# Softmax reciprocals turned once and spread by two transfers, in a cross-attention kernel with a planned order

## The reference

```python
q, k, v = layernorm(x) @ Wq + bq, ctx @ Wk + bk, ctx @ Wv + bv   # 16 heads of 32
sim  = q k^T * 32**-0.5, masked
attn = softmax(sim, axis=-1)
x1   = x + (attn @ v) @ Wo + bo
hn   = layernorm(x1)
p    = softmax(hn @ Ws + bs)                # 4096 tokens x 8 experts
for each expert e: rows = top 512 of p[:, e]
    y = gelu(hn[rows] @ W1[e] + b1[e]) @ W2[e] + b2[e]
    x1[rows] += y * p[rows, e]
```

## Time and profile before

| | us |
|---|---|
| Median of 3 timed runs | 1693.4 |
| The runs | 1683.93, 1697.06, 1693.4 |
| The profiled execution | 1688.73 |
| Its span | 1686.9 |
| Its mean granted TensorE clock | 0.982 |

### The profile page before, as it was taken

How to read it: one execution, slowest core, us unless ns; L and a number is a source line. 1 busy time by engine, 2 the same in 40 slices (tenths; PEclk the granted TensorE clock), 3 DMA queues, 4 the chain that set the end, 5 groups by cost and what they waited for, 6 DMA issues and landing times.

```text
span 1686.9 us, 22363 instructions
## 1 busy us (share of the span) xinstructions
PE 1601.5 (95%) x7847; PEld 1164.9 (69%) x7847; DVE 1113.7 (66%) x1950; ACT 978.3 (58%) x2115; POOL 301.6 (18%) x396
## 2 busy tenths in 40 slices
PE   7999999999999999999976899999999999999997
PEld 5556566666666666666543687888888888888885
DVE  7676968868778697786845667775455545454543
ACT  5898898988989889798863123222232323232321
POOL 6220311312213122130300100102020202020100
PEclk9999999999999999999987999999999999999999
DMA  5543654635446364463611231525253425333430
GB/s 176 172 136 112 188 142 139 189 100 183 145 137 191 95 188 145 133 188 94 189 54 63 83 118 56 164 88 156 100 156 99 134 99 154 103 112 123 109 114 25
DMA packets 131271, 217.27 MB, mean 129 GB/s; under 512 B 17116, under 2 KB 51056, under 8 KB 131160
## 3 DMA queue, kind: packets, MB, share of 16 engines
q1 hardware_dynamic: 114520, 173.23, 32.6%
q0 software_dynamic: 16640, 42.61, 9.3%
HBM read 157.45 MB, written 57.82 MB: 128 GB/s over the span
## 4 chain that ended last, share of the span: by engine, by line
PE 82%; DVE 7%; DMA 4%; ACT 4%; issue 2%; POOL 0%; SPq 0%; DVEq 0%; POOLq 0%; ACTq 0%
PE ps_gen L886 9%; PE ps_gen L887 8%; PE ps_gen L888 8%; PE ps_gen L2067 7%; PE ps_gen L2069 7%; PE ps_gen L2068 7%; PE ps_gen L1903 7%; PE ps_gen L1871 6%; PE ps_att L1914 6%; PE ps_gen L1853 3%; PE ps_gen L1854 3%; PE ps_gen L1855 3%; ACT ps_gen L1278 2%; PE ps_gen L1930 2%; PE ps_gen L1931 2%
## 5 line engine op out<-in xcount | busy, mean ns | idle before, releaser
L1474 DVE TENSOR_REDUCE nmax<-ps_gen 128x1 f32<-128x512 f32 x512 | 330.0, 683 | 78.6 <-PE ps_gen L1871 76.7
L1290 ACT ACTIVATE p_ring<-ps_gen,keep_scale 128x512 f32<-128x512 f32 x512 | 337.7, 701 | 57.8 <-PE ps_gen L1903 47.7
L1278 ACT ACTIVATE ps_gen<-ps_gen,nmax 128x512 f32<-128x512 f32 x512 | 343.3, 680 | 28.6 <-DVE nmax L1474 28.1
L1347 ACT ACTIVATE gel<-ps_gen,b_cols 128x512 f32<-128x512 f32 x128 | 88.3, 690 | 448.8 <-PE ps_gen L888 448.7
L1735 DVE TENSOR_TENSOR gel_lo<-gel,gel_hi 128x512 fp32r<-128x512 f32 x126 | 87.3, 692 | 281.6 <-ACT gel_hi L1348 281.6
L1903 PE MATMUL ps_gen<-qst,kst 99*128 99x512 f32 x512 | 196.8, 425 | 10.7 <-DMA qst<-by_row 9.5
L1871 PE MATMUL ps_gen<-kst,qst 97*128 97x512 f32 x512 | 186.6, 423 | 17.9 <-DMA qst<-qk_rows 7.8
L886 PE MATMUL ps_gen<-hT_hi,w_hi 128*128 128x512 f32 x512 | 202.2, 395 | 0.1
L888 PE MATMUL ps_gen<-hT_hi,w_lo 128*128 128x512 f32 x512 | 199.5, 390 | 0.0
L887 PE MATMUL ps_gen<-hT_lo,w_hi 128*128 128x512 f32 x512 | 199.4, 389 | 0.0
L2067 PE MATMUL ps_gen<-w_hi,gel_hi 128*128 128x512 f32 x504 | 198.1, 393 | 0.0
(11 more groups left out here) (218 smaller groups left out, 2671.2 us busy)
## 6 DMA issues: line engine op xcount, KB each, us to landing
w_raw<-in_L_ffn_W SPq DMA_DIRECT2D x128, 512.0 KB, 5.0
kst<-qk_rows SPq DMA_DIRECT2D x93, 256.0 KB, 4.0
qst<-qk_rows SPq DMA_DIRECT2D x93, 256.0 KB, 3.8
x_in<-in_x POOLq DMA_DIRECT2D x60, 256.0 KB, 3.9
out_x<-x_in SPq DMA_DIRECT2D x32, 256.0 KB, 3.2
qk_rows<-kT_hi SPq DMA_DIRECT2D x31, 256.0 KB, 2.0
qk_rows<-kT_lo SPq DMA_DIRECT2D x31, 256.0 KB, 3.5
qk_rows<-qT_hi SPq DMA_DIRECT2D x31, 256.0 KB, 2.0
```

What stands on the lines that cost most here:

```text
L1278: e.activation(psum[:, :], psum[:, :], ACT.Exp, bias=nmax[g % 2][:, c], scale=-1.0, accum_out=den[g % 2][:, c]).then_inc(drained_sem("max" ...
L1290: e.activation(p_ring[n % NP_][:, :], ps("score", g, kt, h)[:, :], ACT.Exp, scale=keep_scale[:, b:b + 1]).then_inc(drained_sem("score", g, ...
L1474: e.tensor_reduce(nmax[g % 2][:, h * TB + t:h * TB + t + 1], ps("max", g, h, t)[:, :], AX.X, ALU.min).then_inc(s_min, 1)
```

## The change

- `recip` ends with VectorE's reciprocals of 128 x 16. `rden_wide` and GpSimd's spread are gone.
- `rden` is one transpose of 128 x 16 to 16 x 128. ScalarE, not VectorE, copies it, as 16 rows, to `rden_rows` (partitions 64 to 79 of `by_row`).
- SP gets two new steps: `den_out` stores the 16 rows in HBM (`den_rows`, 8 KB), `den_in` loads them into `rden_b` (128 x 512), where each of 4 heads' rows of 512 goes to 32 partitions. `den_in` waits for `den_out` to land and for the division of the group before.
- `divide` multiplies `ps_att` by `rden_b` and waits for `den_in`. It also takes over the wait for the split of the group before.
- `piece_in` is due at `NG - 1` and needs the last stacks and the last maximum rows in the plan. In SP's program its own semaphore waits are the same.
- Planner: some costs are 1% higher, maximum rows are reckoned at 3.2 instead of 2.6 us, `LOOK` is 0, and nearly all due times and lags are new.

```diff
-           "att": (1.105, 1.15), "v": (2.74, 2.94), ...
+           "att": (1.120, 1.17), "v": (2.78, 2.98), ...
-    "pe": {"proj": (0.693, 0.89), "max": (0.231, 0.43), "rows": (0.109, 0.31), "rden": (0.436, 0.63), ...
+    "pe": {"proj": (0.700, 0.90), "max": (0.235, 0.43), "rows": (0.109, 0.31), "rden": (0.109, 0.31), ...
-    "pool": {"rows_lo": (1.050, 2.60), "recip": (0.560, 0.66), ...
+    "pool": {"rows_lo": (1.050, 3.20), ...
+             "den_out": (0.360, 2.40), "den_in": (0.360, 3.60), ...
-LOOK = 0.023
+LOOK = 0
...
-K_AT = ((0.24, 0.248), (-0.055, 0.281), (0.094, 0.256), (-0.698, -0.096))
-Q_AT = ((0.472, 0.472), (0.34, 0.351), (0.109, 0.318), (0.248, 0.412))
-MAX_AT = ((0.124, 0.67), (0.036, 0.694), (-0.083, 0.753), (0.309, 0.742))
-ROWS_AT, RECIP_AT, RDEN_AT, OSPLIT_AT, ATT_AT = 0.132, 0.197, 0.833, -0.55, 0.042
+K_AT = ((0.261, 0.362), (-0.04, 0.247), (0.044, 0.207), (-0.373, -0.096))
+Q_AT = ((0.442, 0.468), (0.192, 0.352), (0.222, 0.42), (0.384, 0.511))
+MAX_AT = ((0.015, 0.674), (-0.097, 0.585), (-0.024, 0.954), (0.091, 0.741))
+ROWS_AT, RECIP_AT, RDEN_AT, OSPLIT_AT, ATT_AT = -0.78, 0.558, 0.153, -0.175, 0.093
...
-            p.add("pool", ("recip", g), g + RECIP_AT, [("dve", "recip", g), ("pe", "rden", g - 1)])
-        p.add("dve", ("rden", g), g + RDEN_AT, [("pe", "rden", g), ("dve", "osplit_lo", g - 1)], frees=("rden", g))
+        p.add("act", ("rden", g), g + RDEN_AT, [("pe", "rden", g), ("sync", "den_out", g - 1)], frees=("rden", g))
+        p.add("sync", ("den_out", g), g + RDEN_AT, [("act", "rden", g), ("sync", "den_in", g - 1)])
+        p.add("sync", ("den_in", g), g + RDEN_AT, [("sync", "den_out", g), ("dve", "divide", g - 1)])
...
-        p.add("dve", ("divide", g), g + 1, [("pe", "att", g, KT - 1), ("dve", "rden", g)])
+        p.add("dve", ("divide", g), g + 1, [("pe", "att", g, KT - 1), ("sync", "den_in", g), ("dve", "osplit_lo", g - 1)])
...
+    stacked = [("sync", "stack_" + k, w, NG - 1) for k in ("hi", "lo") for w in "kq"] + [("pool", "rows_lo", NG - 1)]
     for n in range(3):
-        p.add("sync", ("piece_in", n), NG - 2, done)
+        p.add("sync", ("piece_in", n), NG - 1, done + stacked)
...
+                elif kind == "den_out":
+                    g, = at
+                    on.wait_ge(*drained("rden", g))
+                    if g > 0:
+                        on.wait_ge(s_den_in, 16 * g)
+                    e.dma_start(den_rows, rden_rows).then_inc(s_den_out, 16)
+
+                elif kind == "den_in":
+                    g, = at
+                    on.wait_ge(s_den_out, 16 * (g + 1))
+                    on.wait_ge(s_nrm, g)
+                    src = den_rows.rearrange("(h d t) n -> h d (t n)", d=1, t=TB).to_broadcast([HG, DH, S])
+                    e.dma_start(rden_b[:, :], src).then_inc(s_den_in, 16)
...
+                elif kind == "rden":
+                    g, = at
+                    on.wait_ge(*full("rden", g))
+                    if g > 0:
+                        on.wait_ge(s_den_out, 16 * g)
+                    e.activation(rden_rows, ps("rden", g)[0:HG * TB, 0:P], ACT.Copy).then_inc(drained_sem("rden", g), 1)
...
-                    e.tensor_copy(att_n[:, :], ps("rden", g)[:, :]).then_inc(drained_sem("rden", g), 1)
...
-                    e.tensor_tensor(att_n[:, :], ps_att[:, :], att_n[:, :], ALU.mult).then_inc(s_nrm, 1)
+                    e.tensor_tensor(att_n[:, :], ps_att[:, :], rden_b[:, :], ALU.mult).then_inc(s_nrm, 1)
...
-                    on.wait_ge(s_rden_wide, g + 1)
-                    for t in range(TB):
-                        last = e.transpose(ps("rden", g)[:, t * P:(t + 1) * P], rden_wide[:, t, :], ident[:, :])
-                    last.then_inc(full_sem("rden", g), 1)
+                    on.wait_ge(s_rden, g + 1)
+                    e.transpose(ps("rden", g)[0:HG * TB, 0:P], rden[:, :], ident[:, :]).then_inc(full_sem("rden", g), 1)
```

More of the change, by code:

```diff
@@ L351 @@
 COST = {
[L352 to L355, removed]
+    "pe": {"proj": (0.700, 0.90), "max": (0.235, 0.43), "rows": (0.109, 0.31), "rden": (0.109, 0.31), "score": (0.235, 0.43),
+           "att": (1.120, 1.17), "v": (2.78, 2.98), "turn": (0.436, 0.63), "outa": (1.395, 1.60), "osum": (0.700, 0.90),
+           "out": (1.395, 1.60), "route": (0.436, 0.63), "logits": (0.405, 0.52), "back": (0.109, 0.31)},
+    "act": {"proj": (0.585, 0.73), "sum": (0.662, 0.82), "rows": (0.174, 0.30), "rden": (0.174, 0.30), "score": (0.570, 0.72), "osplit": (0.613, 0.79),
             "csplit": (0.520, 0.66), "turn": (0.477, 0.64), "logits": (0.157, 0.31), "route": (0.477, 0.64),
             "choice_exp": (0.136, 0.26), "wsplit": (0.585, 0.72)},
-    "dve": {"proj_lo": (0.658, 0.78), "max": (0.600, 0.72), "rows_lo": (0.313, 0.32), "recip": (0.160, 0.30), "rden": (0.597, 0.72),
+    "dve": {"proj_lo": (0.658, 0.78), "max": (0.600, 0.72), "rows_lo": (0.313, 0.32), "recip": (0.160, 0.30),
             "divide": (0.592, 0.72), "osplit_lo": (0.659, 0.78), "v": (0.570, 0.72), "csplit_lo": (0.600, 0.72),
@@ L362 @@
             "choice": (0.540, 0.60), "wsplit": (0.660, 0.78), "tables": (0.500, 0.60)},
[L363 removed]
+    "pool": {"rows_lo": (1.050, 3.20), "load": (0.550, 4.00), "load_wo": (0.550, 3.30),
              "residual": (0.550, 4.00), "stats": (0.600, 0.75), "add_bias": (1.240, 1.39), "out": (0.600, 0.75),
@@ L372 @@
 LAG = {
[L373 to L376, removed]
@@ L377 @@
-    ("act", "csplit"): -0.079, ("pe", "rows"): 0.166, ("dve", "route"): -0.071, ("dve", "max"): -0.081, ("dve", "recip"): -0.034,
-    ("act", "score"): 0.027, ("act", "sum"): 0.034, ("pe", "score"): -0.219, ("dve", "osplit_lo"): 0.15,
-}
-K_AT = ((0.24, 0.248), (-0.055, 0.281), (0.094, 0.256), (-0.698, -0.096))
-Q_AT = ((0.472, 0.472), (0.34, 0.351), (0.109, 0.318), (0.248, 0.412))
-MAX_AT = ((0.124, 0.67), (0.036, 0.694), (-0.083, 0.753), (0.309, 0.742))
-ROWS_AT, RECIP_AT, RDEN_AT, OSPLIT_AT, ATT_AT = 0.132, 0.197, 0.833, -0.55, 0.042
+    ("act", "proj"): -0.031, ("dve", "proj_lo"): 0.06, ("pool", "rows_lo"): -0.421, ("act", "rows"): 0.237, ("dve", "rows_lo"): -0.317,
@@ new lines @@
+    ("sync", "stack_hi"): 0.667, ("sync", "stack_lo"): 0.695, ("dve", "outa"): -0.613, ("dve", "csplit_lo"): 0.348, ("dve", "turn_lo"): -0.134,
+    ("dve", "v"): -0.252, ("dve", "out"): 0.295, ("act", "turn"): 0.002, ("dve", "back"): 0.19, ("act", "osplit"): -0.471,
+    ("dve", "divide"): 0.548, ("act", "logits"): -0.534, ("pool", "add_bias"): -0.598, ("act", "csplit"): -0.111, ("pe", "rows"): 0.596,
+    ("dve", "route"): -0.208, ("dve", "max"): -0.068, ("dve", "recip"): 0.075, ("act", "score"): 0.166, ("act", "sum"): 0.034,
@@ L386 @@
-    "stats": (-3, 0.587, 0.597), "norm": (-3, 0.577, 0.856), "turn": (-3, 0.676, 0.826), "residual": (2, -0.159, 0.515),
-    "add_bias": (2, 1.445, 2.219), "outa": (2, 0.138, 0.992), "out": (4, 0.006, 0.738), "x1_norm": (4, 0.603, 1.647),
-    "route": (4, 0.389, 1.208), "logits": (4, 0.608, 1.2), "back": (4, 0.751, 1.343),
+    "v": (-1, 0.319, 1.753), "load_c": (-3, -0.86, 0.048), "csplit": (-3, -0.448, -0.433), "load_x": (-3, 1.249, 1.325),
+    "stats": (-3, 0.527, 0.578), "norm": (-3, 0.62, 1.209), "turn": (-3, 0.054, 0.228), "residual": (2, 0.694, 1.292),
@@ L389 @@
+    "add_bias": (2, 2.317, 3.554), "outa": (2, 0.087, 1.061), "out": (4, 0.054, 0.794), "x1_norm": (4, 0.837, 1.213),
+    "route": (4, 0.459, 1.179), "logits": (4, 0.561, 1.237), "back": (4, 0.736, 1.063),
 }
@@ L561, in attention_moe_kernel @@
 def attention_moe_kernel(nc, x, ctx_T, mask, Wq, bq, Wk, bk, Wv, bv, Wo, bo,
-                         Ws, bs, W1, b1_T, W2, b2, out, hn_rows, mask_rows, qk_rows):
+                         Ws, bs, W1, b1_T, W2, b2, out, hn_rows, mask_rows, qk_rows, den_rows):
     ROW = hn_rows.shape[1]
@@ L1488, in vector_program @@
                     if g > 0:
-                        on.wait_ge(s_rden_wide, g)
+                        on.wait_ge(*full("rden", g - 1))
                     e.reciprocal(rden[:, :], den[g % 2][:, :]).then_inc(s_rden, 1)
-                elif kind == "rden":
+                elif kind == "divide":
                     g, = at
-                    on.wait_ge(*full("rden", g))
+                    b, c4 = divmod(g, GB)
+                    on.wait_ge(s_av, KT * (g + 1))
+                    on.wait_ge(s_den_in, 16 * (g + 1))
                     if g == 0:
```

32 lines of the change are left out of this document (11 added, 21 removed).

## The result

The change made the kernel slower: a median of 1710.25 us in 7 runs beside 1689.97 us of before, ratio 1.0118 with a 95% interval of 1.0098 to 1.0139. The prediction was 1670, range 1655 to 1685, and faster. The profiled execution of after took 1716.57 us; it is the longest of its seven (1704.07 to 1716.57).

The account below looks back on a forecast made before the run. TensorE was taken as the bound, ScalarE in the last groups. Terms -9.3, -3, -9.5 and +0.5 sum to -21.3, from 1688.7 to 1667.4 us, or 1672.1 with the timed runs' difference; the middle, 1670, was forecast, range 1655 to 1685.

Parts of the forecast that it names:

- What is added: ScalarE's 32 copies and SP's small store and 256 KB load per group: +0.5 us, bounds 0 and +60.
- Rival C: The load on SP's queue delays a coming group's stacks, 2 us in each of 30 groups: 1730 us; chance 0.06.
- The rule that was weighed: SP's load, with 4 as slowest dimension, would run on 4 of 16 engines: 4.3 us estimated, sum unchanged.
- Transposes, -9.3: One TensorE transpose of the reciprocals instead of four, groups 0 to 28: -9.3 us, bounds 0 and -10.3.
- Weights behind the last stacks, -9.5: Experts' first weights issued behind group 31's stacks: TensorE's 7.8 us wait there goes; -9.5 us in all, bounds 0 and -13.
- The planner's numbers and the freed engines, -3: New queue order, with VectorE's copy and GpSimd's spread gone, shortens TensorE's waits: -3 us, bounds -15 and +12.
- Rival A: The hole at 841 us moves instead of closing: weights meet group 31's small store and load; 1676 us, chance 0.12.
- Rival B: ScalarE, with its added copies, or the new order takes the saving back: 1682 us; chance 0.22.

## Why the prediction was wrong

- **What failed: "What is added", the term +0.5.** By the version with four loads and the changed kernel (ratios 0.9818 and 1.0118) the load on few engines costs 0.030 or 51 us. The prediction had the right place, a load on SP in front of a coming group's stacks, and bounds up to +60, and took +0.5. Three steps led there. I asked first whether the load is in time for its own division; it always was. I then took it that the stacks "landed in time everywhere but once" and so had slack; slack against 2.0 us for a store says nothing about 8.34. And I priced the lanes by the load's own duration, estimated at 4.3 us from the page of the Trainium skill named below, with 2.3 us of delay for a transfer behind it. The load took 6.4 us in the median, and the six stores before the stalls took 3.4 us longer than at the same place before. Both are about one and a half times the estimate.
- **What was missing is the chain behind the load.** In the place at 219 us the query's stack loads wait for this store, the key's lo load stands behind them on SP, and once issued they run beside other transfers and land late as well. The query's lo part took 8.58 us in after, and 4.58 in the version with four loads. TensorE waited at the end of that chain.
- **Rival C, with 0.06, was the one that came.** That its size was 50 us for the forecast 60 is in part luck. C had 2 us in each of 30 groups; what came were waits of 2.6 to 7.2 us once in a batch, and a slower clock.
- **The price is a stall and the clock after it.** The waits before maxima are 31.9 us and 3.4 in the version with four loads, 28.5 us apart. To these come stretches at the lower clock, as in 219 to 224 us. For the same 7751 matmuls TensorE is busy for 1602.7 us in after and 1581.7 in the version with four loads, 21.0 us more at a mean granted clock of 0.971 beside 0.988. Together that is 49.5 of the 56.8 us between the two profiled spans (1714.5 and 1657.7). That the clock falls behind such a stall stood in the earlier trace rows, and rival C had not counted it.
- **The rule that was weighed.** The Trainium skill (DMA: Bandwidth & Descriptors, Why a DMA increments its semaphore by 16 and not by 1) ties the number of engines to the slowest dimension of both sides. The runs agree with it in order and in kind: slowest dimension 2, 4, 8 and 32 or 128 gave 1766, 1706 to 1710, 1670 and 1660 us. They agree in number too: 2, 4, 8 and 16 updates come from the data of one such transfer. That each of these is one engine's is the rule's reading; no row here names an engine. The prediction cited the rule and then let it change nothing in the sum; that was the mistake.
- **Transposes, -9.3.** Measured 6 to 8 us, with an interval that holds 9.3. Right in kind; their busy time is 10.5 us, so some of it seems to hide in TensorE's waits.
- **Weights behind the last stacks, -9.5.** Measured 6.6 and 6.8 us in two orders, the second not clear of noise. The wait of 7.8 us went as said. Over the whole span the clock gave nothing back: its mean is 0.981 with the weights moved alone and 0.982 before.
- **The planner's numbers and the freed engines, -3.** The new numbers alone cost 21 us and the new steps under the old numbers cost 21 us too (1.2% each), both together with four loads gain 31. They are one change, not two, and the bound of +12 was too small for either alone. With the two measured terms (7.9 and 6.8) taken from the 31 us gained, about 16 us are left for the order together with the engines' relief, where I had said 3. Some 10 of them are TensorE's busy time: with the same 7847 matmuls it is 1601.5 us before and 1591.2 in the run with four transposes. Why its clock holds better there, and how the rest divides, is open.
- **Rival A** did not come: the division of the last group was not held by the load. **Rival B**: ScalarE has 718.7 us in 50 to 830 us of the version with four loads, 92%, and TensorE is as busy as before (755.7 us, was 756.6); so its copies are hidden there.

The sum of -21.3 fits neither kernel: with the load spread the measured gain is 31 us, and with the load as it was changed there is a loss of 20.

## What to carry to other kernels

Before a transfer is given to a shared queue, look at the slowest dimension of both its sides, and ask who is queued behind it and who waits for that, not only whether its own user can wait. A broadcast of a few rows to many partitions is better cut into one transfer per row, so that each has many partitions as its slowest dimension; here the three more issues were free and the cut was worth 3%. Where a planner orders the queues, its numbers and its steps are tested together: each alone lost 1.2% here.

## What was not expected of the hardware

256 KB per group on top of half-busy DMA engines cost nothing when spread (1659.7 beside 1659.9 us with 8 KB), and 51 us when gathered on few. The DMA share over the whole stretch hardly tells the two apart: 0.51 in the slow kernel, 0.55 in the fast one. A mean over 16 engines hides that a few of them are the bound. What tells them apart is how many updates a transfer makes on its semaphore: 16 where it is spread, and one more than its slowest dimension where that is 2, 4 or 8.

The views show this only as a blank. They gave a landing time for the load wherever its slowest dimension was 32 or more (2.2 to 3.1 us), and none where it was 2, 4 or 8. A blank alone proves nothing, though. The experts' weights (`w_raw`) have none in after and none in the version with four loads either. There the trace kept fewer updates than 16 for each transfer, and where it kept all, the view gives 4.5 to 5.0 us.
